# Deformable convolution, sampling stage: strips written out, a second patch buffer, another opening, tap steps spread over the strip, residual added on VectorE

## The reference, cut to what matters

```
B, H, W, C, DG, K = 4, 64, 64, 256, 8, 3                 # all float32
fine     = group_norm(x, 32 groups)
attn     = sigmoid(mean(fine) @ attend_w)
fine_cal = (fine * (attn + 1)) @ select_w
coarse_up = resize(coarse, (B, H, W, C), 'bilinear')
om   = conv3x3(concat([fine_cal, 2 * coarse_up]) @ offset_w, om_w) + om_b
off, mask = om[..., :144], sigmoid(om[..., 144:])          # 8 groups x 9 taps x 2, 8 x 9
val  = bilinear samples of coarse_up at (pixel + tap + off), times mask   # B,H,W,9,C
out  = x + relu(val @ dcn_w + dcn_b) + fine_cal
```

## Time and profile before

| | |
|---|---|
| median of three runs | 3216.22 us (3210.22 to 3219.1) |
| the profiled execution: time, span | 3217.3 us, 3215.5 us |
| PE, PEld busy | 3030.1 us (94%), 2633.8 us (82%) |
| DVE, ACT, POOL busy | 2518.1 us (78%), 1519.0 us (47%), 335.7 us (10%) |
| costliest lines of PE | 1556: 1219.1 us; 1114: 700.2 us; 548: 593.1 us |
| mean granted clock of PE | 0.971 |

### The profile page before, as it was taken

The page is one execution under the profiler, slowest core; times in us unless marked ns, Lnnn a source line. Parts: engine busy times, 40 slices in busy tenths (PEclk is TensorE's granted clock), DMA queues, the critical chain, the costliest instruction groups (busy, mean ns, idle before and its releaser), DMA issues.

```text
span 3215.5 us, 90885 instructions
## 1 busy us (share of the span) xinstructions
PE 3030.1 (94%) x33906; PEld 2633.8 (82%) x33906; DVE 2518.1 (78%) x4299; ACT 1519.0 (47%) x2787; POOL 335.7 (10%) x445
## 2 busy tenths in 40 slices
PE   7799999999999828999998999998999998999999
PEld 7689999989999826888887888887888887888887
DVE  5448888878888849888886888887888886888881
ACT  0122222222222116666665666665666665666662
POOL 2000000000000001111111111111111111111110
PEclk9889999999999959999999999999999999999999
DMA  6333244324434232233223232223223223222221
GB/s 212 103 109 64 54 69 64 60 43 64 60 51 50 31 62 45 56 65 63 54 62 60 61 58 62 62 55 69 54 62 66 54 61 61 61 55 65 62 60 50
DMA packets 452627, 207.13 MB, mean 64 GB/s; under 512 B 230820, under 2 KB 447540, under 8 KB 452276
## 3 DMA queue, kind: packets, MB, share of 16 engines
q1 hardware_dynamic: 426112, 161.74, 28.6%
q10 hardware_dynamic: 21724, 26.37, 2.5%
q0 software_dynamic: 4608, 16.78, 1.4%
HBM read 104.86 MB, written 55.23 MB: 50 GB/s over the span
## 4 chain that ended last, share of the span: by engine, by line
PE 52%; ACT 6%; issue 3%; DVE 1%; ACTq 1%; SPq 1%; DMA 0%; POOL 0%; POOLq 0%; DVEq 0%
PE eb L1556 29%; PE tb L1114 15%; PE vb L1136 6%; ACT taps_all L1085 2%; ACT res L1143 2%; ACT wtT L1119 1%; ACT om L1041 1%; PE eb L1149 1%; PE tb L1036 1%; ACT mask L1050 1%; ACTq L1007 1%; DVE wt L1108 0%; SPq L1031 0%; DMA rt<-r_d 0%; DMA om_s<-om_d 0%
## 5 line engine op out<-in xcount | busy, mean ns | idle before, releaser
L1556 PE MATMUL eb<-val,wd 128*128 128x256 f32 (+1 forms) x4680 | 1219.1, 384 | 0.0
L1119 ACT COPY wtT<-tb 128x512 f32<-128x512 f32 x1152 | 663.6, 588 | 607.8 <-PE tb L1114 606.3
L1556 PEld LDWEIGHTS eb<-val,wd 128*128 128x128 f32 x4680 | 794.6, 190 | 121.2 <-issue 57.3
L1108 DVE TENSOR_TENSOR wt<-taps_all 128x768 f32<-128x768 f32 x768 | 731.7, 994 | 10.4 <-PE tb L1114 2.1
L1114 PE MATMUL tb<-ident,wt 128*128 128x128 f32 x4608 | 700.2, 275 | 34.6 <-ACT wtT L1119 18.8
L1114 PEld LDWEIGHTS tb<-ident,wt 128*128 128x128 f32 x4608 | 560.8, 141 | 178.2 <-ACT wtT L1119 59.3
L548 PE MATMUL conv<-fine,wf 128*108 128x256 f32 x4608 | 593.1, 289 | 14.5 <-DVE omT L879 14.5
L548 PEld LDWEIGHTS conv<-fine,wf 128*108 128x108 f32 x4608 | 572.4, 173 | 30.5 <-issue 30.5
L1136 PE MATMUL vb<-wtT,win 64*32 64x144 f32 x16384 | 318.4, 289 | 39.7 <-issue 33.3
L1489 DVE COPY val<-vb 128x432 f32<-128x432 f32 (+1 forms) x384 | 212.7, 554 | 143.4 <-PE vb L1136 143.0
L1136 PEld LDWEIGHTS vb<-wtT,win 64*32 64x32 f32 x16384 | 241.9, 106 | 83.3 <-issue 83.3
(11 more groups left out here) (138 smaller groups left out, 2320.7 us busy)
## 6 DMA issues: line engine op xcount, KB each, us to landing
val<-val SPq DMA_DIRECT2D x128, 396.0 KB, 3.8
win<-cpad SPq DMA_DIRECT2D x304, 64.0 KB
om_s<-om_d SPq DMA_DIRECT2D x1152, 12.0 KB
chunk<-in_x SPq DMA_DIRECT2D x32, 512.0 KB, 6.0
xchunk<-in_x SPq DMA_DIRECT2D x32, 512.0 KB, 3.9
r_d<-r POOLq DMA_DIRECT2D x32, 512.0 KB, 3.2
rt<-r_d SPq DMA_DIRECT2D x63, 256.0 KB, 4.9
out<-ot ACTq DMA_DIRECT2D x63, 256.0 KB, 2.2
```

Of the source, the lines that this page charges most:

```text
L1108: return nc.vector.tensor_tensor(wt[b][:, PER * d:PER * (d + 1), WQ * u:WQ * (u + 1)].rearrange("p k (a b) -> p k a b", a=WIN), of_rows(0) ...
L1119: return nc.scalar.copy(dst, src) if e == "act" else nc.vector.tensor_copy(dst, src)
L1556: done = nc.tensor.matmul(eb[q][:, 256 * fo:256 * fo + rows], wd[:, half, k, 128 * fo:128 * fo + 128], val[:, half, k, at:at + rows // W, ...
```

## The change

- `strips written out`: `loop` on PE, ACT and DVE has no loop any more; all 34 double strips are written out. SP and POOL keep loops.
- A second patch buffer `win1`: image b uses `wins[b % 2]`. The 16 transfers of the next image are issued before strip 12 of the image before (`whole_windows`), all at once; the first strip of an image no longer loads anything.
- Opening: the constants are loaded by ACT. SP loads the half-0 offsets of strip 0, ACT those of half 1, and then ACT loads `dcn_w`. ACT does `keep` for strip 0, the tap steps of strip 0, then `keep` for strip 1. DVE caps and multiplies half 0 of strip 0 and caps half 1 before it turns to strip 1.
- The tap steps are split into `tap_lengths` (line 1085) and `tap_slopes` (line 1087): half 0 after batches 0 and 3 of half 0, half 1 after batches 3 and 5 of half 1. DVE's `cap` of half 1 goes behind `locate` and `measure` of the strip after.
- `add_rest` moves from POOL to DVE, in half 1, ahead of the second third of the products.

```diff
-        win_all = sb("win", [128, 2 * BLK * 128])
-        win = win_all[:].rearrange("p (j c) -> p j c", c=128)
+        win_both = [sb(f"win{i}", [128, 2 * BLK * 128]) for i in range(2)]
+        wins = [t[:].rearrange("p (j c) -> p j c", c=128) for t in win_both]
+        win_all, win = win_both[0], wins[0]
...
-        def tap_weights(act, q, chain, start):
+        def tap_lengths(q, chain):
             nc.scalar.activation(tap[q], tap[q], ACT.Abs).then_inc(chain, 1)
+        def tap_slopes(act, q, chain, start):
             act.wait_ge(chain, start + 1)
             nc.scalar.activation(tap[q], tap[q], ACT.Identity, bias=k34[:], scale=-0.5).then_inc(chain, 1)
...
+            LENGTHS_AT, SLOPES_AT = (0, 3), (3, 5)
...
             def loop(e, strips):
-                strips(0)
-                strips(1)
-                with e.Fori(2, ST // 2 - 1) as it:
-                    strips(it)
-                for it in range(ST // 2 - 1, ST // 2 + 2):
+                for it in range(ST // 2 + 2):
                     strips(it)
...
+                def whole_windows(b):
+                    w(sp, "sampled", 6 * SI * (b - 1))
+                    windows(b, b * (PADC * PADC * C), range(WIN), sems["win_whole"])
...
                     w(sp, "sampled", 6 * s)
-                    if turn is None:
-                        windows(at, range(2, WIN), sems["win_first"])
-                        h(sp, "win_first", 16 * 12 * (b + 1))
-                        windows(at, range(0, 2), sems["win_ready"])
-                    else:
+                    if turn is not None:
...
-                load_offsets(sp, 0, True, sems["om_loaded"])
+                load_offsets(sp, 0, True, sems["om_loaded"], (0,))
                 for s in range(1, 3):
                     w(sp, "batched", s)
                     load_offsets(sp, s, True, sems["om_loaded"])
...
+                whole_windows(0)
+                for b in range(B):
                     opening(b)
-                    with sp.Fori(1, 4) as m:
+                    with sp.Fori(1, 3) as m:
                         four(b, 4 * m)
+                    if b + 1 < B:
+                        whole_windows(b + 1)
+                    four(b, 12)
...
@@ pool_fast
-                        add_rest(t - 2)
...
@@ act_fast, slot
-                        if hx == 0 and i == 5:
-                            taps(t + 1, 1 - p, 0)
+                        if i == LENGTHS_AT[hx]:
+                            lengths(t + 1, 1 - p, hx)
+                        if i == SLOPES_AT[hx]:
+                            slopes(t + 1, 1 - p, hx)
...
                             keep(t + 2, batch_no(t, 0, NT), bank_no(t, p, 0, NT))
-                        taps(t + 1, 1 - p, 1)
...
-                for s in range(2):
-                    keep(s, s, s)
+                load_offsets(act, 0, True, sems["om_loaded"], (1,))
+                load_weights(act)
+                act.wait_ge(consts, CONSTS)
+                keep(0, 0, 0)
                 for hx in range(2):
-                    taps(0, 0, hx)
+                    lengths(0, 0, hx)
+                    slopes(0, 0, hx)
+                keep(1, 1, 1)
...
@@ dve_fast
+                def add_rest(s):
+                    if known(s, 0, ST + 1):
+                        m = W if isinstance(s, int) and s == ST else 256
+                        w(dve, "finished", 2 * (s + 1))
+                        w(dve, "r_ready", 16 * (s + 1))
+                        nc.vector.tensor_tensor(res[:, :, 0:m], res[:, :, 0:m], rt[:, :, 0:m], ALU.add
+                                                ).then_inc(sems["summed"], 1)
...
                     for d in range(3):
+                        if hx == 1 and d == 1:
+                            add_rest(t - 2)
                         third(*half_after(t, p, hx), d)
                         keep_values(*half_before(t, p, hx), d)
...
-                        cap(t + 1, 1 - p, 1)
                         locate(t + 2, p)
                         measure(t + 2, p, 0)
+                        cap(t + 1, 1 - p, 1)
...
+                cap(0, 0, 0)
+                products(0, 0, 0)
+                for d in range(3):
+                    third(0, 0, 0, d)
+                cap(0, 0, 1)
                 dve.wait_ge(sems["dist_ready"], 4)
                 locate(1, 1)
                 dve.wait_ge(sems["pchain"], 2 * NPOS)
                 measure(1, 1, 0)
-                for hx in range(2):
-                    cap(0, 0, hx)
-                products(0, 0, 0)
-                for d in range(3):
-                    third(0, 0, 0, d)
...
@@ pe_fast, first_runs
                         if hx == 0:
-                            w(pe, "win_ready", loaded)
+                            w(pe, "win_whole", 16 * 16 * (s // SI + 1))
+                            w(pe, "win_ready", 64 * (s // SI * (SI - 1) + s % SI))
```

More of the change, by code:

```diff
@@ L1016, in sample_and_project, with load_offsets @@
         OM_LOADS = 2 * NK
-        def load_offsets(e, s, shifted, signal):
+        def load_offsets(e, s, shifted, signal, halves=range(2)):
             at = (s // SI) * ((NOM * HP - SI * 4) * HP) + s * (4 * HP)
@@ L1026, in load_offsets @@
                 c = TAPC * (k % 5)
-                for hx in range(2):
+                for hx in halves:
                     src = bass.AP(tensor=om_d.tensor,
@@ L1126, in bank_of, with sample_blocks @@
             return vb[u][v % 2][:, 0:NK * 4 * m].rearrange("p (k y x) -> p k y x", k=NK, y=4)
-        def sample_blocks(half, v, window):
+        def sample_blocks(half, v, window, win):
             for j in range(*THIRDS[v]):
@@ L1160, in fast @@
             names = ("om_loaded masked pchain coef_ready dist_ready achain capped products batched tb_out based "
-                     "win_first win_ready sampled kept_near kept_far cleared sides entered crossed ready projected finished "
+                     "win_whole win_ready sampled kept_near kept_far cleared sides entered crossed ready projected finished "
                      "r_ready summed turned ob_out out_stored duplicated").split()
@@ L1221, in duplicate_rows, with windows @@
                                      ).then_inc(sems["duplicated"], 16)
-                def windows(at, rows, signal):
+                def windows(b, at, rows, signal):
                     for a in rows:
@@ L1234, in strip @@
                     p = 0 if turn is None else turn % 2
-                    at = b * (PADC * PADC * C)
                     w(sp, "sampled", 6 * s)
-                    if turn is None:
-                        windows(at, range(2, WIN), sems["win_first"])
-                        h(sp, "win_first", 16 * 12 * (b + 1))
-                        windows(at, range(0, 2), sems["win_ready"])
-                    else:
-                        at = at + 2 * (i - turn) * (PADC * C)
+                    if turn is not None:
+                        at = b * (PADC * PADC * C) + 2 * (i - turn) * (PADC * C)
                         if not isinstance(at, int):
                             at = sp.snap(at)
-                        windows(at, range(2 * turn + 6, 2 * turn + 8), sems["win_ready"])
+                        windows(b, at, range(2 * turn + 6, 2 * turn + 8), sems["win_ready"])
                     if known(s - 2, 0, ST):
@@ L1377, in keep, with lengths, slopes @@
                     sigmoid().then_inc(sems["masked"], 1)
-                def taps(s, p, hx):
+                def lengths(s, p, hx):
                     if known(s, 0, ST):
-                        n = 2 * s + hx
-                        w(act, "dist_ready", 2 * (n + 1))
-                        tap_weights(act, 2 * p + hx, sems["achain"], 2 * n)
+                        w(act, "dist_ready", 2 * (2 * s + hx + 1))
+                        tap_lengths(2 * p + hx, sems["achain"])
+                def slopes(s, p, hx):
+                    if known(s, 0, ST):
+                        tap_slopes(act, 2 * p + hx, sems["achain"], 2 * (2 * s + hx))
                 def keep_values(s, p, hx, v):
```

49 lines of the change are left out of this document (16 added, 33 removed).

## The result

The changed kernel takes 3137.74 us, the median of four runs (3131.0 to 3141.09), against 3213.3 us of the kernel before timed with it: ratio 0.976, 95% interval 0.9737 to 0.9784. Timed again beside its variants it takes 3131.46 us, ratio 0.9739 (0.9717 to 0.9762). The profiled execution takes 3136.0 us, its span is 3134.3 us; the forecast was 3128, its range 3113 to 3158. The median lies inside the range, 9.7 us above the forecast.

What follows compares the result with a forecast made beforehand. PE was taken as the bound, busy 59.63 of 60.00 us. Terms 41.7 + 38 + 8 + 1 = 88.7 us gave 3128.6 in the profiled execution's terms, 3127.5 as a median, stated as 3128; range 3113 to 3158.

Steps and rivals of the forecast that it cites:

- the tap steps: ACT between batch copies: single steps fit where two did not, so PE's 0.70 us a strip returns; 41.7 us, bounds 20 to 42.
- the boundaries: Image boundaries: with a second patch buffer the three long intervals become ordinary; 38 us, low bound 26.
- the opening: Start of the stage: offsets out 4 to 6 us sooner, half 0's products before `locate`; 8 us, bounds 2 and 14.
- the end: Last two strips: the residual add stands in the chain and is 0.6 us shorter on DVE; 1 us.
- an undisturbed strip: PE's interval without delay: 29.29 us near the end plus 0.38 for the offset turn, 29.67 against 30.37 present.
- unwaited they cost SP its issue time only: SP queue before strip 12: 16 patch transfers cost only issuing, 0.45 us each; 25 and 16 take 18 us of 30.
- a rival at 12 us: Boundaries give only part, as 1 MB of patches delays strip 12: 12 us lost, 3140 us, chance 8%.
- lose the wait between the 12 and the 4: Opening: the first image's patches no longer wait after 12 transfers before 4 more; part of the opening's 8 us.
- the contention of the two engines: DVE products and POOL's add block each other: 0.57 us on one side, 0.65 on the other.
- bound 3 us: Strips written out: costed at nothing, upper bound 60 times the 0.05 us seen in one written-out interval.
- slow streaming: PE's code between batches: instructions stream too slowly; 250 us if 213 packets are wholly exposed, 3378 us, chance 5%.
- costly loop ends: Loop back edges cost 1.2 us at each of 29, which writing out saves: 34 us, 3094 us, chance 3%.

Runs made afterwards that it cites:

- changed kernel again: The changed kernel run once more, unaltered, beside its variants (also called the repeat): 3131.46 us, ratio 0.9739 to the kernel before.
- first image's patches early: Changed kernel with the first image's 16 patch transfers issued ahead of strip 2's offsets instead of behind them: 3129.18 us, ratio 0.9734 to the kernel before.
- add back on GpSimd: Changed kernel with the residual add (`add_rest`) moved back from DVE to POOL: 3127.76 us (3120.78 to 3140.92).
- rows ahead of the burst: Changed kernel with the 16 patch transfers issued inside strip 12, behind its two rows and residual rows, ahead of its offsets: 3127.34 us, ratio 0.9735.
- patches spread: Changed kernel with the next image's 16 patch transfers issued four behind each of strips 12 to 15: 3126.51 us, ratio 0.9724 to the kernel before.
- one patch buffer: Changed kernel with all patches in `win0`, the next image's 16 transfers issued unwaited after the last strip's sampling: 3163.45 us.
- tap steps alone: Kernel before with only the tap steps split and spread, half 1's cap behind locate and measure, loops kept: 3177.57 us against 3216.66, ratio 0.9889.
- opening alone: Kernel before with only the opening changed, tap steps left in pairs: 3209.69 us against 3216.8, ratio 0.9982.

## Why the prediction was right, and where a term was off

The sum of 88.7 us was 41.7 for the tap steps, 38 for the boundaries, 8 for the opening and 1 for the end. Measured between the two spans are 41.7, 28.6, 5.2 and 3.8, less 0.8 for small stretches in a few intervals, and 2.8 us by which the stage began earlier, which is chance. So 13 us were missing, and the early start, which is luck, and 2.8 us more at the end than I had foreseen made up 5.5 of them. Without these two it is 75.7 us, and the medians differ by 75.6.

**Tap steps: right in mechanism and size.** I took an undisturbed strip of 29.67 us from one interval near the end, less the offset turn, and that is the interval measured to the hundredth. The experiment with this part alone gives 39 us where the sum had 41.7. That a single step fits between two copies and a pair does not, holds: the weight loads' wait of 59.3 us for copies is gone, and the matmuls' own falls from 12.9 us to 0.8.

**Second buffer: right that the three long intervals become ordinary, off on what the burst does.** The step that failed is "unwaited they cost SP its issue time only", and with it "the queue behind them holds the two rows for strip 12, the residual rows and the offsets; all have several us of slack". The term of 38 us came to 28.6. The queue of SP in the changed kernel and PE's timeline behind it:

```profile
1539.46 13.84 SPq L1230 DMA_DIRECT2D win<-cpad  x20
1553.35 0.77 SPq L1266 DMA_DIRECT2D rt<-r_d  x1
```

```profile
1557.40 0.60 PE L1118 MATMUL tb<-ident,wt 128*128 128x128 f32 x4
1562.14 3.14 PE L1140 MATMUL vb<-wtT,win 64*32 64x144 f32 x96 [4.14 <-issue]
```

The 20 transfers are the 16 and the 4 of strip 12. Issuing them took 0.69 us each where I had 0.45, and SP still had the time. The data had not: the four land after 1558.0, when PE wants them. PE idles 4.14 us and then samples at the lower clock, 3.14 us for what takes 1.73 elsewhere; the granted clock from 1562 to 1567 us is 0.50, that is 1.2 GHz. Together 6.86 us. I had named this as a rival at 12 us; with the 2.47 us of strip 28 it came to 9.3.

The trace has the landings of the four transfers as events of the semaphore that PE waits for (`win_ready`). For strip 12, in us:

```
                               first of the     the four    PE starts   strip 12
                                  20 issues       landed     sampling      takes
changed kernel                      1539.46    1561.94      1562.14       36.53
changed kernel again                1539.44    1561.81      1562.01       36.54
first image's patches early         1533.86    1552.19      1552.51       29.68
add back on GpSimd                  1537.89    1554.58      1556.62       29.67
rows ahead of the burst             1543.87    1550.10      1552.09       29.85
```

Where the strip is long, PE starts 0.20 us after the last landing. Behind the burst the four land 16.7 to 22.5 us after its first issue, and PE wants them after some 18.5, so it can go either way; ahead of it they land 6.2 us after their own first issue. That shows the cause. What makes the same burst take 16.7 us in one execution and 22.5 in another stays open. Of the four profiled executions with the burst ahead of the rows, strip 12 was long in two and strip 28 in three.

In strip 28 the place is another. PE stands still in the middle of a batch of four, while the burst of 2020.11 to 2035.32 is under way:

```profile
2027.53 0.49 PE L1118 MATMUL tb<-ident,wt 128*128 128x128 f32 x3
2030.32 0.27 PE L1118 MATMUL tb<-ident,wt 128*128 128x128 f32 x1 [2.30 <-issue]
```

No data can be late between the third and the fourth matmul of a group, so I read it as PE's instructions being late. The packets of PE's instruction queue q8 bear that out: one starts at 2011.62 us and the next only at 2027.51, and PE goes on 2.8 us after that. Between 1280 and 3060 us and outside the image boundaries, the packets are at most 14.1 us apart in all ten runs with written-out strips, but for five places of 14.5 to 17.0 us, and at each of the five PE stood still for 1.87 to 3.75 us. Three are strip 28 behind the burst; the other two are near the end, with patches spread and with one patch buffer, where no burst is near. So the burst may delay a packet, but is not needed for it. What delays it stays open. The three runs that keep the loops (before, tap steps alone, opening alone) have no stop for `issue` above 0.25 us outside the boundaries; seven of the ten with strips written out have one to four, not counting strip 12's wait for data.

**Opening: 8 predicted, 5.2 measured (5.7 in the repeat, 6.5 with the opening alone).** The first sampling was forecast at about 1204 us and is at 1203.61, but that match is luck: the stage began 2.76 us earlier. Counted from its start the sampling comes after 49.82 us, 5.6 less than the 55.43 of before. The step that failed is again that the patches "lose the wait between the 12 and the 4": from their first issue to the sampling it is 19.8 us, before 18.6. The rows of the changed kernel, from the timelines of SP, ACT and PE, against the earlier trace rows:

```profile
1183.85 9.12 SPq L1230 DMA_DIRECT2D win<-cpad  x16
```

```profile
1188.62 1.16 ACT L1086 ACTIVATE taps_all<-taps_all 128x1152 f32<-128x1152 f32 x1 [8.86 <-DVE taps_all L1081]
```

```profile
1203.61 3.14 PE L1140 MATMUL vb<-wtT,win 64*32 64x144 f32 x96 [4.22 <-DMA win<-cpad]
```

Both obstacles that I named are there: the lengths of strip 1 hold ACT for 8.86 us, though taking that wait away gains nothing, and the patches hold PE for 4.22. The second costs twice, since PE then samples at the lower clock. In two variants with this very opening (patches spread, rows ahead of the burst) the patches came 2.6 to 3.2 us earlier, PE's wait was 1.5 and 0.9 us, and the first marker 112.06 and 111.43 us after the start. So the opening has two outcomes some 5 us apart, decided by when the patches land: of six executions with this order of transfers four took 116.9 to 117.9 us, and three with the first image's patches early all took 111.9 to 112.3. Much of the spread from 3131 to 3141 us may be that.

**Add on DVE: right.** 0.68 us as the estimate had it, nothing on the path, and 0.8 us at the end where 1 was forecast, with one execution on each side. The rows bear out the contention of the two engines, since the 2.39 us pair is gone, but PE never felt it.

**Strips written out: nothing predicted, bound 3 us, 3.5 measured (0.6 to 6.8).** The bound had been read from a single interval, 0.05 us above the others, and with the tap steps in pairs it held in nearly every one of them. In the changed kernel that price isn't there, 29.67 us written out as in a loop; what is left are the stops told above. The rivals of slow streaming and of costly loop ends are both out at the sizes that I gave them. As to the Trainium skill (Runtime: NRT & Kernel Launch, Instruction fetch mechanics), fetching is mostly hidden here, as it says, with stops of 0.3 to 3.75 us at one to four places of a run, but the gain from full unrolling isn't there.

The end of the run is 3.8 us shorter than before where I had 1. At the third result turn from the end PE was idle in the kernel before, since POOL's add had waited for residual rows, and a lower clock followed (0.88 from 3190 to 3204 us):

```profile
3190.00 0.66 PE L1149 MATMUL eb<-ident,res 128*128 128x128 f32 x4 [2.41 <-POOL res L1341]
3190.49 14.42 PE L1556 MATMUL eb<-val,wd 128*128 128x256 f32 x72
```

Now the 72 take 12.74 us. In the three runs that keep the loops this idle time is 2.4 to 2.9 us; in the two with strips written out and the add on GpSimd it is 1.0 and 1.1, and the last three intervals are 40.52 and 40.46 us against 43.5. So the rest of the gain goes along with the written-out strips, in one execution of each kernel. Why the residual rows land sooner there stays open.

## What to carry to other kernels

When PE is the bound, look for the interval of its loop in which the suspected work is missing; here one such interval at the end, plus the one piece of work that must come back, gave the new period exactly. A prefetch has two costs, the queue's issue time and the time until the data behind it lands, and the second is what counts: put the small transfer that is wanted next ahead of the large one, or send the large one in pieces. An idle gap of PE can cost more than its length, since the work behind it may run at the lower clock: one of 4.14 us cost 6.86 here. Profile more than one execution before giving a cause to a long interval: here the same order of transfers had it in some executions and not in others.

## What the runs showed of the hardware that was not expected

- At an image boundary 1 MB of patches in 16 transfers needs 17.6 to 19.9 us from first issue to use with the issuing done after some 9 us, and 18.2 to 20.9 with a wait after the twelfth transfer.
- Written-out code makes the steady interval 0.05 us longer than the same code in a loop (30.42 and 30.37 us) with the tap steps in pairs, and no longer (29.67 and 29.67) with them spread.
- PE's stops of 1.87 to 3.75 us in written-out code fall on the only places among the steady strips where its instruction queue brought no packet for more than 14.1 us.
- After idle gaps of 4.14, 4.22 and 11.57 us the same 96 sampling matmuls take 3.14 us instead of 1.73; after a gap of 0.91 us they take 1.72. The length of the gap alone doesn't decide: after the stop of 3.75 us in strip 28 (add on GpSimd) the granted clock is 1.00 from 2026 to 2031 us and the strip is 3.90 us longer, and 72 projecting matmuls take 14.42 us after a gap of 2.41 in the kernel before, but 12.74 after one of 2.92 with the tap steps alone.
